# Graph network on one core: the last pairs of the edge MLP and the bank ring of the last layer

## The reference

```python
# third layer: MLP over the edges, then over the nodes
edge_feat = concatenate([x[src], x[dst], edge_attr])
h = mish(edge_feat @ W1 + b1)
messages = mish(h @ W2 + b2)
agg = segment_sum(messages, dst)
u = mish(concatenate([x, agg]) @ W3 + b3)
y = x + (u @ W4 + b4)
out = layernorm(y) * gamma + beta
# fourth layer
m_ij = relu(concatenate([x[src], x[dst]]) @ W.T + b)
out = segment_sum(m_ij, src)
```

## Time and profile before

| what | value |
| --- | --- |
| median of 3 runs | 1168.77 us (1164.44, 1169.74, 1168.77) |
| profiled execution, its own time | 1167.43 us |
| its span | 1165.6 us |
| PE, PEld, DVE, ACT, POOL busy | 93%, 50%, 73%, 48%, 43% |
| mean granted PE clock | 0.976 |
| edge MLP's last products, from 946.7 | to 952.5 us |
| last layer's loop on PE | 1049.45 to 1159.3 us |

### The profile page before, as it was taken

How to read it: one execution, slowest core, us unless ns; L and a number is a source line. 1 busy time by engine, 2 the same in 40 slices (tenths; PEclk the granted TensorE clock), 3 DMA queues, 4 the chain that set the end, 5 groups by cost and what they waited for, 6 DMA issues and landing times. The chain is left out here.

```text
span 1165.6 us, 15308 instructions
## 1 busy us (share of the span) xinstructions
PE 1082.5 (93%) x4358; PEld 588.0 (50%) x4358; DVE 856.0 (73%) x2016; ACT 557.9 (48%) x978; POOL 498.8 (43%) x434
## 2 busy tenths in 40 slices
PE   3779888899999988999999999999999989999997
PEld 1133223344557453755555555555555547446664
DVE  5997667769755153787887887887887856848997
ACT  0221321311332311577777777777777734115564
POOL 0000112243333430768876666666666200027773
PEclk9788989999999999899999999999999999999999
DMA  7996997657111005685554444444444020026665
GB/s 281 366 361 229 362 379 272 229 186 248 63 50 46 13 14 193 143 251 112 115 105 99 97 96 99 96 97 98 97 97 76 2 74 3 9 84 202 210 211 160
DMA packets 60183, 172.65 MB, mean 148 GB/s; under 512 B 12646, under 2 KB 13190, under 8 KB 52553
## 3 DMA queue, kind: packets, MB, share of 16 engines
q0 software_dynamic: 31536, 72.01, 26.3%
q1 hardware_dynamic: 28568, 99.66, 23.2%
HBM read 159.65 MB, written 11.98 MB: 147 GB/s over the span
## 5 line engine op out<-in xcount | busy, mean ns | idle before, releaser
L1630 PE MATMUL PS<-wide,hidT 128*128 128x512 f32 x672 | 302.1, 592 | 0.0
L689 POOL DMA_INDIRECT rec_scratch<-rec_src,slot_row x84 | 99.0, 1179 | 262.5 <-DMA rec_scratch<-rec_src,slot_row 211.9
L1630 PEld LDWEIGHTS PS<-wide,hidT 128*128 128x128 f32 x672 | 128.6, 191 | 122.8 <-issue 120.5
L1566 ACT ACTIVATE wide<-PS 128x512 f32<-128x512 f32 x168 | 100.3, 597 | 100.5 <-PE PS L1616 64.2
L1453 POOL DMA_INDIRECT pair_sum<-table_j,counts_rec x84 | 136.1, 1620 | 27.6 <-issue 25.3
L1758 POOL DMA_INDIRECT u_space<-table_j,wide x87 | 83.0, 955 | 111.8 <-DMA table_j<-agg_space 84.9
L1445 POOL DMA_INDIRECT pair_sum<-table_i,counts_rec x84 | 89.3, 1063 | 97.1 <-PE PS L1616 59.7
L1571 ACT ACTIVATE wide<-wide,two 128x512 f32<-128x512 f32 x168 | 120.9, 719 | 6.2 <-DVE wide L1504 6.2
L1504 DVE SCALAR_TENSOR_TENSOR wide<-wide 128x512 f32<-128x512 f32 x168 | 116.3, 692 | 5.8
L1576 ACT ACTIVATE wide<-wide 128x512 f32<-128x512 f32 x168 | 105.8, 630 | 5.3
L1462 POOL DMA_INDIRECT rec_scratch<-rec_src,slot_row x84 | 87.5, 1041 | 41.1 <-issue 21.6
(11 more groups left out here) (321 smaller groups left out, 1849.2 us busy)
## 6 DMA issues: line engine op xcount, KB each, us to landing
pieces<-basis_rows SPq DMA_DIRECT2D x56, 1024.0 KB, 7.3
ring<-basis_low SPq DMA_DIRECT2D x30, 256.0 KB, 6.2
w_scratch<-pieces SPq DMA_DIRECT2D x112, 32.0 KB
counts_rec<-rec_scratch SPq DMA_DIRECT2D x1, 2856.0 KB, 9.5
rec_scratch<-rec_src,slot_row POOLq DMA_INDIRECT x168, 2.2
root<-L_gnn_root SPq DMA_DIRECT2D x2, 1024.0 KB, 6.2
rows_in<-in_rows_in SPq DMA_DIRECT2D x2, 1024.0 KB, 15.5
w_rel<-w_scratch SPq DMA_DIRECT2D x1, 2048.0 KB, 11.1
```

Of the source, the lines that this page charges most:

```text
L689: nc.gpsimd.indirect_dma_start(out=rec3_dram, out_offset=bass.IndirectOffsetOnAxis(ap=slot_row[:, 1, t:t + 1], axis=0), in_=rec, in_offset ...
L1566: nc.scalar.activation(grow[l][:, t % 2, :], PS[:, bank, :], ACT.Exp).then_inc(sem(f"exp{l}"), 1)
L1630: m = nc.tensor.matmul(o, hidT[:, t % 2, k * P:(k + 1) * P], w2[:, k, :], start=False, stop=(k == KT - 1), skip_group_check=True)
```

## The change

Edge MLP: the numbers of pairs 83 to 87 are loaded inside messages 81 to 83, behind their third and fourth matmuls, and kept in registers; HOT3 is 5 instead of 2; three of the four last one-hots are made ahead of the last `split_message`. Last layer: the turned one-hots and the own products share one ring of banks 5, 6 and 7 in the order in which PE makes them, each waiting for the reader of the use three back; LAG5 is 4 instead of 3.

```diff
-            GOT3, LAG3, LATE5, HOT3, TURN_GROUP = 9, 3, 8, 2, 4
+            GOT3, LAG3, LATE5, HOT3, TURN_GROUP = 9, 3, 8, 5, 4
@@ DVE, steps of the edge MLP
                     if 0 <= s + 1 < ET:
                         finish_hidden(s + 1)
+                    if s == ET:
+                        for n in range(ET, ET + 3):
+                            one_hot(n)
                     if 0 <= s - 1 < ET:
                         split_message(s - 1)
-                for n in range(ET, PAIRS):
+                for n in range(ET + 3, PAIRS):
                     one_hot(n)
@@ PE, message(t)
+                last_pairs = []
                         if k == 1 and t:
                             chunk = pair_at(t - 1)
+                        if t >= ET - 3 and k in (2, 3) and len(last_pairs) <= PAIRS - ET:
+                            last_pairs.append(pair_at(ET - 1 + len(last_pairs)))
@@ PE, steps
-                        seg_sum(s - 2, chunk if s - 1 < ET else pair_at(s - 2))
+                        seg_sum(s - 2, chunk if s - 1 < ET else last_pairs[0])
                 for n in range(ET, PAIRS):
-                    seg_sum(n, pair_at(n))
+                    seg_sum(n, last_pairs[n - ET + 1])
@@ last layer
-            LAG5 = 3
+            LAG5 = 4
-            TURN_BANK, OWN_BANKS = 5, (6, 7)
+            RING5 = [("turn", 0)]
+            for t in range(NS):
+                if t % TURN_GROUP == 1 and t // TURN_GROUP + 1 < N_TURN:
+                    RING5.append(("turn", t // TURN_GROUP + 1))
+                RING5.append(("own", t))
+            ring_at = {use: n for n, use in enumerate(RING5)}
+            own_bank = lambda t: 5 + ring_at["own", t] % 3
+            turn_bank = lambda j: 5 + ring_at["turn", j] % 3
+                def ring_free(use):
+                    if ring_at[use] >= 3:
+                        kind, n = RING5[ring_at[use] - 3]
+                        if kind == "own":
+                            pe.wait_ge(sem("pair_sum5"), n + 1)
+                        else:
+                            pe.wait_ge(sem("is_srcT"), n + 1)
@@ turn(j)
-                    if j:
-                        pe.wait_ge(sem("is_srcT"), j)
+                    ring_free(("turn", j))
@@ own(t, chunk)
-                    if t >= 2:
-                        pe.wait_ge(sem("pair_sum5"), t - 1)
+                    ring_free(("own", t))
```

More of the change, by code:

```diff
@@ L1841, in add_pair @@
                             dve.wait_ge(sem("sum_lo"), (t - PAIR5) // 2 + 1)
-                    nc.vector.tensor_tensor(pair5[:, t % PAIR5, :], PS[:, OWN_BANKS[t % 2], :], got5[:, t % GOT5, :],
+                    nc.vector.tensor_tensor(pair5[:, t % PAIR5, :], PS[:, own_bank(t), :], got5[:, t % GOT5, :],
                                             ALU.add).then_inc(sem("pair_sum5"), 1)
@@ L1930, in turned @@
                         act.wait_ge(sem("own_mm"), TURN_GROUP * (j - 1))
-                    nc.scalar.copy(is_srcT[:, j % 2, :, :].rearrange("p g e -> p (g e)"), PS[:, TURN_BANK, :]).then_inc(sem("is_srcT"), 1)
+                    nc.scalar.copy(is_srcT[:, j % 2, :, :].rearrange("p g e -> p (g e)"), PS[:, turn_bank(j), :]).then_inc(sem("is_srcT"), 1)
                 for c in range(NT):
@@ L2004, in self_of @@
                     m.then_inc(sem("t40_mm"), 1)
+                def ring_free(use):
[5 more added lines that the diff above has]
+                            pe.wait_ge(sem("is_srcT"), n + 1)
                 def turn(j):
                     pe.wait_ge(sem("is_src5"), TURN_GROUP * (j + 1))
-                    if j:
-                        pe.wait_ge(sem("is_srcT"), j)
+                    ring_free(("turn", j))
                     for g in range(TURN_GROUP):
-                        m = nc.tensor.transpose(PS[:, TURN_BANK, g * P:(g + 1) * P], is_src5[:, (TURN_GROUP * j + g) % HOT5, :].bitcast(F32), ident[:])
+                        m = nc.tensor.transpose(PS[:, turn_bank(j), g * P:(g + 1) * P], is_src5[:, (TURN_GROUP * j + g) % HOT5, :].bitcast(F32), ident[:])
                     m.then_inc(sem("turned"), 1)
@@ L2018, in own @@
                         pe.wait_ge(sem("is_srcT"), t // TURN_GROUP + 1)
-                    if t >= 2:
-                        pe.wait_ge(sem("pair_sum5"), t - 1)
+                    ring_free(("own", t))
                     l = is_srcT[:, t // TURN_GROUP % 2, t % TURN_GROUP, :]
                     for n, part in enumerate((own_hi, own_lo)):
-                        m = nc.tensor.matmul(PS[:, OWN_BANKS[t % 2], :], l, part[:, bass.ds(chunk, 1), :].rearrange("p c o -> p (c o)"),
+                        m = nc.tensor.matmul(PS[:, own_bank(t), :], l, part[:, bass.ds(chunk, 1), :].rearrange("p c o -> p (c o)"),
                                              start=(n == 0), stop=(n == 1))
```

## The result

The first measurement gave 1159.09 us as median of 4 runs (1158.99 to 1161.44), against 1167.97 for the kernel before (4 runs, 1164.44 to 1169.74): ratio 0.9933, 95% interval 0.9905 to 0.9960.

The account below looks back on a forecast made before the run. PE was taken as the bound (93% busy), waiting for loaded numbers at the edge MLP's end and saturated in the last layer. Gains of 2.8 + 1.4 + 0.9 - 0.4 + 0.35 = 5.05 us gave 1163.7 us, range 1160.3 to 1168.0.

Parts of the forecast that it names:

- the allowance for the spread of medians: Whole time: medians of three runs differing by 5 us widen the range by one or two us on the lower side.
- the gathers' zero: Last layer's loop: POOL's gathers of rows run 8 tiles ahead, so they cost zero.
- The chances: Whole time, 0.5% being 5.8 us: faster 0.34, same 0.61, slower 0.05.
- The sum: All edited places together: 2.8 + 1.4 + 0.9 - 0.4 + 0.35 = 5.05 us gained.
- Loads moved: End of edge MLP: without loads between them, products stand 0.56 instead of 1.26 us apart, 2.8 us gained over four distances.
- One-hots at no cost: Edge MLP, DVE: three one-hots fit ahead of the last split, the fourth right behind it; cost zero.
- End of the block moves as a whole: Behind the edge MLP's last product: the 1.45 us with nothing busy stay and move forward, as only PE is late.
- The clock: Block behind the edge MLP: PE busy 77% instead of 48% beforehand keeps full clock, 1.4 us gained, bounds 0 and 1.4.
- Steady part: Last layer's loop: periods of four tiles fall from 5.00 to 4.94 us, PE alone setting the pace; 0.9 us gained.
- The parity argument: Last layer: LAG5 = 4 swaps the product order between own(4q+2) and the turn, giving DVE's closed loop 0.4 us more.
- the rivals on the ring: Last layer: own(4q+3) stalls at each of 21 turns, 1174 us, 5%; or five clock falls in the loop, 1170.7, 1%.
- Start and end of the loop: Last layer: start loses 0.4 us, own(3) waiting for ACT's copy; end gains 0.35 with one more product queued.

Follow-up runs that it names:

- e1: The changed kernel measured again with no edit, against the kernel before: ratio 0.9955, median 1161.36 us of 8 runs.
- e11: Kernel before with five one-hot places and three one-hots made ahead of the last split, loads not moved; no ratio given, last products 1.26 us apart.
- e4: Kernel before with only the five loads moved, two one-hot places as before: ratio 0.9959, last products 0.72 us apart.
- filler: Kernel before plus dummy matmuls, whose result nobody reads, ahead of each of the last four pair loads: ratio 0.9981 with bf16, 0.9982 with f32.
- e7: Kernel before with LAG5 = 4 alone, banks and edge MLP as before: ratio 1.0000.
- e8: Kernel before with the ring of three banks alone, LAG5 = 3: ratio 1.0015.

## Why the prediction was wrong in its range, and which of its steps held

The step that failed is the allowance for the spread of medians in the range. In the sum it is the gathers' zero, which was really a cost of 0.2 us in the first trace (10.23 - 10.01) and 1.0 in e1 (10.97 - 10.01), and the reason given for the clock did not hold. One by one:

- **The range, the step that failed.** "Medians of three runs that differ by 5 us add one or two on the lower side." The runs showed more. The median that I subtracted from, 1168.77, was high: the 93 runs of the kernel before in four later series have a median of 1166.7 (1162.1 to 1173.1), 2.1 lower. And the four runs of the first measurement were low: the 17 of the two repetitions have a median of 1162.6 (1157.1 to 1166.8), 3.5 above 1159.09 and 1.1 below the forecast of 1163.7. Four drawn at random from the 17 have a median of 1159.1 or less about once in twenty. So the number missed by luck in both kernels, of which the first trace shows 3.5 us in code that is the same in both, and the fault of the prediction is to have allowed for so little of it. With 3.3 us on the lower side instead of one or two the range would have begun at 1158.6 (an estimate made afterwards, from these draws).
- **The chances.** Faster by over 0.5% (0.34) was not unfair: the difference is about 0.4% by the edited places (4.8 of 1168 us) and by the repetitions (0.45 and 0.36%), on the near side of the line, and the first measurement fell beyond it.
- **The sum: 5.05 forecast.** Edited places in the trace 4.8, repetitions 5.3 and 4.2.
- **Loads moved: right.** 0.7 us less per distance was forecast, 0.67 measured; 2.70 against 2.8 us. No stall in messages 81 to 83: from product 80 to 81, 81 to 82 and 82 to 83 it is 5.30, 6.51 and 3.70 us, in the kernel before 5.30, 6.51 and 3.71.
- **One-hots at no cost: right** for their place ahead of the split. That they alone give nothing is right too (e11); but the sum let them give nothing with the loads moved either, and there they are worth 0.5 of the 2.7 us (e4).
- **End of the block moves as a whole: right**, 1.5 us before and after.
- **The clock: the result right (1.46 against 1.4 us), the reason not.** I argued from PE's busy share, 77% against 48%. The 77% was itself misread: the matmuls' modelled durations overlap once they stand closer, and the changed kernel has 65%. With filler the share was 72 to 73%, above that, and the clock still fell in three of four traces. What I can stand by is the association with the length of the thin end. Nor is 1.4 us the most that a fall costs here: in e7 and e8, where the granted clock was 0.50 all the way from the block's start to 957.0 us, it took 5.25 us instead of 2.66 from the first u_half to the first transpose.
- **Steady part: right.** 4.94 forecast, 4.929 measured, 1.05 us against 0.9, and the lag is the cause (e7). The parity argument fits, but a lag of 4 also queues one product more, and no run has the longer lag with the old parity. Of the rivals on the ring neither came: the granted clock is 1.00 over the whole loop, and turns 4.929 apart leave no room for a stall of own(4q+3).
- **Start and end of the loop: sizes off.** From the start to the second turn one two-part product (0.46 us) fewer is done, and it takes 5.02 to 5.35 us against 5.12, so it loses 0.4 to 0.7 (forecast 0.4; 0.68 in the changed kernel). The end holds that product more, and without late gathers wins 10.05 + 0.46 - 10.01 = 0.5 (forecast 0.35). In the changed kernel's first trace 10.05 + 0.46 - 10.23 = 0.28 are left, and in e1 it comes to a loss of 0.46. "POOL's gathers run 8 tiles ahead: zero" is the term that failed: it took a lead at the loop's start for one at its end, where the rows land just when they are added, or later.

## What to carry to other kernels

A gap between short matmuls whose addresses come from a loaded register can be the sequencer's, as it was here (1.26 us apart with the load, 0.59 without): look at its own rows (load, register steps, wait) before believing the releaser, then load the numbers under long matmuls. When PE takes over a loop whose other engine issues at nearly the same rate (1.25 against 1.23 us), the next limit is there already; compare rates over the whole loop and not the lead at one moment. And split a difference of two spans by anchors before explaining it: what arises in unedited code is chance until a repetition says otherwise.

## What the runs showed of the hardware

- The same code reaches the same instruction (the edge MLP's first segment product) anywhere from 491.0 to 498.9 us in 17 traces; the 452.4 us from there to product 83 vary by only 0.4.
- A fall of TensorE's clock to 1.2 GHz near one point of the program (1003 to 1008 us) occurs in 4 of 17 traces and costs 1.5 to 1.7 us each.
- Ahead of the block that follows the edge MLP PE has 1.5 us without any matmul. The clock was kept there in all of 8 traces with 3 us of dense segment products before, and lost in 8 of 9 with 6 us of spread ones, even with filler that made PE 91% busy (4.39 of 4.80 us); in e7 it was lost already among the products, at 948.2. The Trainium skill ("TensorE: Matmul & The Clock Gate", Part 1: The HAM clock gate) ties the rate to recent busy-ness of the array; by the busy time in the rows alone that is not enough to tell these cases apart.
- A TENSOR_LOAD with its register steps and assertion holds PE's sequencer for 0.7 us, of which rows show 0.30, 0.15 and 0.02 as busy.
- Indirect gathers of 0.95 us take 1.35 to 1.47 us now and then: in the changed kernel five times in the loop, in the kernel before once. Counting those from 1.08 us up, the traces with a lag of 4 have 5 to 11 in the loop, those with 3 have none to two.
